# Head mixing on one core: scores straight behind each mixing, and VectorE's running sum as the last step of a tile

## What is computed

```
attn = jnp.einsum('bhnd,bhmd->bhnm', q, k) * scale
attn = jax.nn.softmax(attn, axis=-1)
attn = jnp.einsum('gh,bhnm->bgnm', conv_w, attn) + conv_b[None, :, None, None]
mean = attn.mean(axis=(0, 2, 3), keepdims=True)
var = attn.var(axis=(0, 2, 3), keepdims=True)
attn = (attn - mean) * jax.lax.rsqrt(var + BN_EPS)
attn = attn * bn_gamma[None, :, None, None] + bn_beta[None, :, None, None]
out = jnp.einsum('bhnm,bhmd->bhnd', attn, v)
```

## Time and profile before

| what | value |
|---|---|
| median of 3 runs | 4358.7 us (4358.68 to 4359.67) |
| the profiled execution | 4354.42 us |
| its span, first to last instruction | 4352.6 us |
| mean granted clock of TensorE over the span | 0.939 |
| TensorE busy in the span | 3782.2 us (87%) |
| VectorE busy | 2787.5 us (64%) |
| ScalarE busy | 2209.1 us (51%) |
| GpSimd busy | 825.7 us (19%) |

### The profile page before, as it was taken

One profiled execution on the slowest core, in us unless ns is written; L12 is line 12 of the kernel. 1 busy time (PEld: TensorE's weight loads), 2 busy tenths in 40 slices (PEclk: granted clock), 3 DMA queues, 4 the chain that ended last, 5 costly groups with the idle time before them and its releaser, 6 DMA issues. The chain is left out here.

```text
span 4352.6 us, 155594 instructions
## 1 busy us (share of the span) xinstructions
PE 3782.2 (87%) x64620; PEld 2304.4 (53%) x64621; DVE 2787.5 (64%) x5455; ACT 2209.1 (51%) x4201; POOL 825.7 (19%) x2119
## 2 busy tenths in 40 slices
PE   5779999799799997688889759999999999966996
PEld 2357777444477774345555425445545545434763
DVE  5546666311566664578788658878878878863343
ACT  1235555311455552466666527767767767721221
POOL 0000000000000000355555401111111111105023
PEclk7879999899899997899999879999999999988997
DMA  1011111100011111000000021000000000023233
GB/s 52 10 32 48 48 51 50 35 0 0 26 48 48 51 49 62 1 1 1 1 1 1 1 74 35 0 1 1 0 1 1 0 1 0 0 90 116 64 92 113
DMA packets 84608, 131.16 MB, mean 30 GB/s; under 512 B 11440, under 2 KB 67024, under 8 KB 83408
## 3 DMA queue, kind: packets, MB, share of 16 engines
q1 hardware_dynamic: 78288, 111.95, 7.7%
q0 software_dynamic: 6144, 16.79, 1.2%
HBM read 69.98 MB, written 58.72 MB: 30 GB/s over the span
## 5 line engine op out<-in xcount | busy, mean ns | idle before, releaser
L1969 PE MATMUL psum<-hm_ex,hm_mix 128*128 128x512 f32 x1024 | 503.0, 614 | 38.8 <-ACT hm_Aq L2065 38.8
L2051 ACT ACTIVATE hm_ex<-psum,hm_nm 128x1024 f32<-128x1024 f32 x256 | 286.0, 1117 | 255.5 <-DVE hm_nm L2123 255.3
L1969 PEld LDWEIGHTS psum<-hm_ex,hm_mix 128*128 128x128 f32 x1024 | 173.9, 189 | 344.8 <-issue 336.9
L2138 DVE COPY hm_A<-psum 128x1024 f32<-128x1024 f32 x256 | 312.7, 1222 | 54.0 <-PE psum L1978 50.3
L2133 DVE TENSOR_SCALAR_CACHE_REDUCE hm_plus<-hm_Aq,hm_cbcol,hm_sums 128x1024 f32<-128x1024 f32 x256 | 340.3, 1329 | 0.0
L2123 DVE TENSOR_REDUCE hm_nm<-psum 128x1 f32<-128x1024 f32 x256 | 310.7, 1214 | 32.2 <-PE psum L1957 32.2
L1978 PEld LDWEIGHTS psum<-K,hm_Aq 128*128 128x128 f32 x2048 | 236.7, 141 | 149.4 <-issue 139.7
L1529 ACT ACTIVATE pt_signs<-pt_acts,pt_tb 128x1024 f32<-128x1024 f32 (+1 forms) x224 | 227.6, 1018 | 116.0 <-POOL pt_tb L1399 94.9
L2056 ACT ACTIVATE hm_junk<-hm_Aq 128x1024 f32<-128x1024 f32 x256 | 270.6, 1057 | 30.3
L1957 PE MATMUL psum<-hm_kt,hm_qd 64*32 64x512 f32 x4096 | 277.9, 601 | 3.2 <-ACT hm_kt L2074 3.2
L1978 PE MATMUL psum<-K,hm_Aq 128*128 128x128 f32 x2048 | 267.3, 273 | 5.6 <-DVE hm_A L2138 5.6
(11 more groups left out here) (415 smaller groups left out, 7949.7 us busy)
## 6 DMA issues: line engine op xcount, KB each, us to landing
fw_late<-fw_away SPq DMA_DIRECT2D x64, 384.0 KB, 3.1
ex_rows_in<-hm_zero SPq DMA_DIRECT2D x2, 5120.0 KB, 24.2
ex_xs<-ex_rows_in SPq DMA_DIRECT2D x80, 128.0 KB, 2.0
ex_rows_out<-ex_ys SPq DMA_DIRECT2D x80, 128.0 KB, 1.7
fw_away<-fw_kk SPq DMA_DIRECT2D x64, 128.0 KB, 1.8
fw_away<-fw_tr SPq DMA_DIRECT2D x64, 128.0 KB, 1.7
fw_away<-fw_qm SPq DMA_DIRECT2D x64, 128.0 KB, 1.7
ex_w<-in_ex_w SPq DMA_DIRECT2D x2, 4096.0 KB, 19.6
```

The lines of the kernel that those rows point to most:

```text
L1969: mm = pe.matmul(bank[4 + c], mix[:, u, :], ex[:, u, 512 * c:512 * c + 512], start=True, stop=True)
L2051: act.activation(ex[:, u, :], flat2(psum[:, 2 * u:2 * u + 2, :]), ACT.Exp, bias=nm[:, u:u + 1], accum_out=rsum[:, u:u + 1]).then_inc(s_ex, 1)
L2138: dve.tensor_copy(A[:, :, :, QT_ * t:QT_ * t + QT_], flat2(psum[:, 6:8, :]).rearrange("p (m g n) -> p m g n", m=MT, g=HEADS)).then_inc(s_a ...
```

## The change

Both edits are in the two functions `block_of_queries`, of TensorE and of VectorE. TensorE now issues `scores(i+2)` directly behind `mixed(i)`, ahead of the turning and of `values`. VectorE now issues, behind the maxima (and the outputs at t = 1), `evacuate(i-1)`, then `inverse(i+1)`, then `running(i-1)`.

```diff
@@ -1995,14 +1995,14 @@
                             i = n * NQ + t
                             more = not (last and t >= NQ - 2)
                             mixed(i, t % 2, more)
+                            if more:
+                                scores(i + 2, t % 2)
                             if t == 0 and not first:
                                 turn(i - 1, 1)
                             if t == 1 and not first:
                                 values(n - 1)
                             if t > 1:
                                 turn(i - 1, (t - 1) % 2)
-                            if more:
-                                scores(i + 2, t % 2)
                             if t == 1:
                                 if first:
                                     pe.wait_ge(s_v_ev, b * 2 + 2)
@@ -2151,14 +2151,14 @@
                             more = not (last and t == NQ - 1 or first and t == 0)
                             if more:
                                 maxima(i + 1, (t + 1) % 2)
-                            if not (first and t == 0):
-                                running(i - 1, (t - 1) % 2)
-                            if more:
-                                inverse(i + 1, (t + 1) % 2)
                             if t == 1 and not first:
                                 outputs(n - 1)
                             if not (first and t == 0):
                                 evacuate(i - 1, (t - 1) % NQ)
+                            if more:
+                                inverse(i + 1, (t + 1) % 2)
+                            if not (first and t == 0):
+                                running(i - 1, (t - 1) % 2)
```

## The result

| | before | changed |
|---|---|---|
| median of 4 runs each | 4359.18 us | 5095.44 us |
| lowest to highest | 4358.68 to 4365.71 | 5089.45 to 5104.28 |
| profiled execution (its span) | 4354.42 (4352.6) | 5096.01 (5094.2) |
| mean granted clock over the span | 0.939 | 0.903 |

The ratio is 1.168, with a 95% interval from 1.1668 to 1.1696: slower, as forecast, but 110 us above the upper end of the range (4985) and 233 above the forecast (4862). That is the price that the first rival gave (5094).

A forecast was written before the change was run, and what follows sets the result against it. TensorE and VectorE, both nearly full, bound the kernel before; afterwards a four-engine loop of 5.89 us replaces 3.81 per tile. Four batches add 501.8, the end 1.3: +503.1 on 4354.4, plus 4.3, gives 4862 us; range 4825 to 4985.

The forecast's parts named there:

- the first rival: Clock falls repeatedly in head mixing: half of 3.87 us lost in every second of 244 tiles, 232, so 5094; chance 0.13.
- the hand-over: From the end of GpSimd's weights to TensorE's mixing, in each tile: 0.06 us.
- The loop through four engines: In regular tiles each inverse waits for the one before, through weights, mixing, scores, turning and copy: 5.89 us, not 3.81.
- inverse to weights: From VectorE's inverse start to the start of GpSimd's weights: 0.25 us of the loop.
- mixing to copy: TensorE's mixing, scores and turning, up to the start of VectorE's copy: 4.04 us of the loop.
- copy to inverse: On VectorE, from the copy's start to the next instruction: 1.14 us of the loop.
- The tile across the values' product: Tile t = 1 of seven blocks per batch: 10.35 us, 4.46 more than a regular tile.
- the second rival: VectorE's running sum locks out GpSimd's weights: 1.26 us later per tile, 307 over 244 tiles, so 5169; chance 0.03.
- I count no fall in regular tiles: TensorE idles 1.9 us per tile between 128x128 matmuls, yet its clock stays at 1.00; cost 0.
- the other row: Earlier trace: a 2.04 us idle time among 32x32 matmuls, up to 764.99, was followed by clock 0.50.
- GpSimd's end to the matmul that waited for it: Loop step from the end of GpSimd's weights to TensorE's mixing, read at another matmul: 0.06 us.
- The upper bound of 0.15: Longest delay allowed between GpSimd's end and TensorE's mixing, in place of 0.06; the loop would be 5.98 us.

The follow-up runs named there:

- two added matmuls: Changed kernel plus two unread 128x512 matmuls on TensorE behind the turning of each tile that has scores; 4916.06 us.
- the shorter hand-over alone: Changed kernel with the mixing's waits for masked queries and exponentials, two of its four, left out; 5090.39 us.
- fewer waits and two added matmuls: Changed kernel without the mixing's waits for masked queries and exponentials, plus two unread matmuls behind the turning; 4870.29 us.
- VectorE's half alone: Kernel before with only VectorE's new order (copy, inverse, running sum), scores still behind the turning on TensorE; 4656.09 us, ratio 1.068.

## Why the prediction was right in direction and wrong in size

The change costs 736 us. Against the forecast of +503 it leaves 233: 179 are the clock (the change against two added matmuls), 46 the hand-over, and 8 the rest. In the stage itself, by the profiles, the same three are 178, 39 and 5. The parts hang on the order in which they are taken: with the shorter hand-over alone the kernel gains 5, since more tiles are struck then, and the clock is 220.

**What held.** The loop through four engines is what the change does. The forecast's steps beside those of the full-clock tile above: inverse to weights 0.25, measured 0.23; weights 0.40 and 0.40; mixing to copy 4.04 and 4.03; copy to inverse 1.14 and 1.15. The tile across the values' product was to take 10.35 and takes about 10.4. The kernel with both errors taken out of it (fewer waits and two added matmuls) shows the sum itself. GpSimd's weights took 0.40 beside the running sum and started 0.23 behind the inverse, so the second rival (a lock) is out; that is also the exemption which the Trainium skill (SBUF — State Buffer, Who interferes with whom) states for the form with an accumulator. One row was read wrongly there, without harm: in the earlier trace rows the running sum is the second of the two passes beside GpSimd's copy, and the first is a copy from PSUM.

**The step that failed** is the clock: "The turning and the mixing on both sides of the gap are of the first kind, so I count no fall in regular tiles." This took one row, the idle time of 2.11 up to 1834.08, for a rule about a kind of matmul. A gap that once was followed by 1.00 shows that a fall needn't come, not that it doesn't. The trace of before has a row against it, with 128x128 matmuls on both sides of an idle time of 1.93 and the lower level 1.2 us later (the last line has the columns of the earlier trace rows):

```profile
3899.76 2.38 PE L2350 MATMUL psum<-K,H 128*128 128x128 f32 x16
3904.06 0.49 PE L2356 MATMUL psum<-ex_mask,ex_before 128*128 128x128 f32 x2 [1.93 <-DVE ex_mask L2484]
...
3905.30:3908.50 3.20, 0.54 (x4) 0.14 (x1) 2.89 (x16) 0.00 (x0) 0.00 (x0) 0.50 0.92 399
```

After the change, with an idle time of about 2 us ahead of nearly every mixing, 105 of the 242 tiles counted above were struck. The first rival, which had the other row, was the true case and should have had far more than 0.13. The Trainium skill (TensorE: Matmul & The Clock Gate, HAM oscillation) describes kernels whose clock swings because TensorE idles between groups of matmuls; the trace agrees, with 112 low stretches behind gaps of some 2 us, shorter than the waits for DMA that the page has.

The first rival's price agreed less well than it looks. It had half of 3.87, 1.9 us, on every second of 244 tiles, 232 in all. Measured were 1.63 on 105 tiles, 171 to 179 us, since the lower level covered little more than the mixing; the hand-over, which that rival did not have, made up most of the rest. That its 5094 met the measured 5095 is luck.

**The term that was mis-sized** is "GpSimd's end to the matmul that waited for it", 0.06 by the earlier trace rows. That matmul isn't the mixing, and has fewer waits. Measured: 0.25 to 0.30 in most tiles; 0.10 in 48 tiles (t = 0 and 1 of the blocks in the hardware loop, where the code has four waits as well), and 0.06 in the 8 tiles that close a batch, whose mixing has two waits. The upper bound of 0.15 was too low as well.

**What is not settled:** which tiles are struck, and why the gap at 1834 was not followed by a fall. The runs show only this: in the head mixing of all ten kernels every low stretch begins between 1.0 us before and 1.4 us after the end of an idle time of TensorE of 1.86 us or more; about half of these idle times have one in the changed kernel and in the one with fewer waits, fewer in the others; and idle times of up to 1.41 us have none. Nothing between 1.41 and 1.86 occurs. Why the hand-over is 0.10 in the 48 tiles is open too.

## What to carry to other kernels

Look in the order of each engine for a step that waits for another engine's answer to the step before it: moved behind such a wait, a short instruction (0.15 us here) ties four engines into one loop, and the loop's length, not the busiest engine's work, is the tile. When a change leaves TensorE idle for about 2 us again and again, price the fall of its clock as a likely case, not as a tail (in the changed kernel it came at about every second such time; idle times of 1.20 us brought none); added matmuls in the gap tell in one run what it costs. To gain at a stall, move ahead the very step that the stalled chain waits for (the maxima here, 27 us less).

## What the runs showed of the hardware that was not expected

- The clock fell in nearly every second tile behind idle times of about 2 us, though before it had once stayed up behind 2.11. It fell as well where such an idle time came about once in a block: 15 of 36 in the run with VectorE's half alone. A shorter idle time did not bring fewer falls: with 1.86 there were 133 low stretches, with 2.06 there were 112.
- A mixing that waits for GpSimd starts 0.25 us behind GpSimd's end with four waits (0.10 in 48 tiles) and 0.05 to 0.06 with two, in the same place and for the same data. Before the change the weights ended 0.45 us ahead of the mixing, so GpSimd was not on the path there.
- Added work made the kernel faster: 496 added matmuls took 179 us off the changed kernel, and half as many 189.
